# The last stage of a four-layer network: the first weighted addition moved from VectorE to ScalarE and GpSimd

## The reference

```python
xf = layernorm(x).reshape(T, d)                          # T = 4096 tokens, d = 256
shared = silu(xf @ Sg) * (xf @ Su) @ Sd
probs = softmax(xf @ Wr); topk_p, topk_i = top_k(probs, 2)
routed = sum over the two chosen experts e of topk_p * (silu(xf @ Wg[e]) * (xf @ Wu[e]) @ Wd[e])
x = x + routed + shared
```

## Time and profile before

| What | us |
|---|---|
| Median of three executions | 1652.86 (1652.83 to 1653.16) |
| The profiled execution's own time | 1644.97 |
| Its span, from first to last instruction | 1643.2 |
| The last stage in it, from SP's first load to the end | 1587.25 to 1643.2 |
| VectorE busy in the span | 1018.6 |
| ScalarE busy in the span | 736.6 |
| GpSimd busy in the span | 572.3 |

### The profile page before, as it was taken

One profiled execution on the slowest core, in us unless ns is written; L12 is line 12 of the kernel. 1 busy time (PEld: TensorE's weight loads), 2 busy tenths in 40 slices (PEclk: granted clock), 3 DMA queues, 4 the chain that ended last, 5 costly groups with the idle time before them and its releaser, 6 DMA issues. The chain is left out here.

```text
span 1643.2 us, 31228 instructions
## 1 busy us (share of the span) xinstructions
PE 1487.4 (91%) x9905; PEld 1114.3 (68%) x9905; DVE 1018.6 (62%) x3468; ACT 736.6 (45%) x1544; POOL 572.3 (35%) x994
## 2 busy tenths in 40 slices
PE   5999999983999999699799999999999597589987
PEld 3776676772999999565566666666666386468876
DVE  3345555453444444499898888888886286645558
ACT  3444444430222222345177777777777242244420
POOL 4123333344222222245532332322333165635530
PEclk9999999986999999899899999999999798889999
DMA  7001111115777777668857666667761575745556
GB/s 234 1 26 36 49 46 52 39 58 157 212 212 213 212 212 212 211 229 259 203 75 98 98 90 90 92 89 98 98 89 40 143 240 187 171 129 156 161 159 220
DMA packets 150592, 221.74 MB, mean 135 GB/s; under 512 B 23648, under 2 KB 98144, under 8 KB 150304
## 3 DMA queue, kind: packets, MB, share of 16 engines
q1 hardware_dynamic: 127904, 170.58, 45.2%
q0 software_dynamic: 13344, 36.55, 6.4%
q10 hardware_dynamic: 9184, 12.61, 2.5%
HBM read 141.16 MB, written 78.25 MB: 134 GB/s over the span
## 5 line engine op out<-in xcount | busy, mean ns | idle before, releaser
L2095 ACT ACTIVATE t_probs<-t_ps_st 128x512 f32<-128x512 f32 x576 | 313.2, 597 | 124.9 <-PE t_ps_st L2147 122.4
L2073 DVE CUSTOM_DVE_ANT_0 whole_sum<-t_ps_s,t_later 128x512 bf16<-128x512 f32 (+3 forms) x512 | 285.5, 586 | 14.0 <-PE t_ps_s L2133 11.9
L2049 POOL TENSOR_SCALAR_AFFINE_SELECT t_probs<-t_probs 128x128 f32<-128x128 f32 x512 | 137.4, 300 | 330.5 <-ACT t_probs L2095 328.9
L2133 PE MATMUL t_ps_s<-t_ks,t_qs 96*128 96x512 f32 (+3 forms) x768 | 247.8, 362 | 0.5 <-ACT t_neg_max L2085 0.5
L2147 PE MATMUL t_ps_st<-t_qs,t_ks 128*128 128x512 f32 (+3 forms) x768 | 242.7, 365 | 0.8 <-ACT t_probs L2095 0.8
L2147 PEld LDWEIGHTS t_ps_st<-t_qs,t_ks 128*128 128x128 f32 x768 | 136.8, 189 | 73.6 <-ACT t_probs L2095 40.2
L2073 DVE CUSTOM_DVE_ANT_0 whole_sum<-t_ps_s,t_later,t_first_max 128x512 bf16<-128x512 f32 (+3 forms) x256 | 140.5, 549 | 47.8 <-PE t_ps_s L2133 47.8
L2162 PE MATMUL t_ps_o<-t_probs,t_vs 128*17 128x256 f32 (+1 forms) x2560 | 154.9, 361 | 0.5 <-ACT whole_sum L2102 0.5
L2133 PEld LDWEIGHTS t_ps_s<-t_ks,t_qs 96*128 96x128 f32 x768 | 138.7, 190 | 18.0 <-DVE t_first_max L2073 1.6
L1460 POOL DMA_INDIRECT outputs_dram<-m_y,m_place x71 | 68.1, 959 | 208.8 <-DVE m_place L1535 201.1
L1490 PE MATMUL m_ps_h<-m_xt,m_w_t 128*128 128x128 f32 x1136 | 140.7, 278 | 0.0
(11 more groups left out here) (340 smaller groups left out, 2652.1 us busy)
## 6 DMA issues: line engine op xcount, KB each, us to landing
m_w_t<-in_w_dram SPq DMA_DIRECT2D x71, 512.0 KB, 4.4
t_qs<-qkt_dram SPq DMA_DIRECT2D x128, 128.0 KB, 5.6
t_ks<-qkt_dram SPq DMA_DIRECT2D x128, 128.0 KB, 5.7
m_x_t<-gathered_dram SPq DMA_DIRECT2D x79, 128.5 KB, 2.1
m_x_t<-gathered_dram SPq DMA_DIRECT2D x71, 129.0 KB, 2.1
d_ye<-outputs_dram SPq DMA_DIRECT2D x8, 1024.0 KB, 8.2
qkt_dram<-d_hi ACTq DMA_DIRECT2D x32, 256.0 KB, 5.2
qkt_dram<-d_lo SPq DMA_DIRECT2D x32, 256.0 KB, 7.2
```

Source lines behind the costliest of these rows:

```text
L2049: nc.gpsimd.affine_select(out=diag, in_=diag, compare_op=ALU.is_ge, fill=0.0, base=0, pattern=[[1, P]], channel_multiplier=-1).then_inc(ma ...
L2073: nc.vector.tensor_tensor_reduce(out=seen[:, (NP * p + x) % (RS + 1), 0:keys], in0=bank_of(p, x)[:, 0:keys], in1=masks, scale=1.0, scalar= ...
L2095: nc.scalar.activation(probs[:, p % 2, i // NST, base:base + STC], ps_st[(NX * p + i) % RT][:], ACT.Exp, scale=HD ** -0.5).then_inc(exp_re ...
L2133: nc.tensor.matmul(bank_of(p, x)[:, 0:keys], q[0:MAX_ROW, head, qc * P:(qc + 1) * P], k[0:MAX_ROW, head, k0:k0 + keys], start=True, stop=T ...
```

## The change

ScalarE multiplies the first expert's rows of every group by their probability, in place in `ye`, one ACTIVATE (Copy with a scale per partition) per tile: 32 in all. GpSimd, which gets an instruction list in this stage, adds the two tiles' products to `total` in one instruction of 128x512 per group: 16 in all. VectorE has the 32 instructions of L2683 no more; its second additions wait for GpSimd's sum of the same group in the place of the loads and of its own first additions. ScalarE's list is sigmoid k, products of the plain group k, products of the shared group 8 + k - 1.

```diff
--- before.py
+++ after.py
@@ -2648,6 +2648,7 @@
     ps_y = [pb(f"f_ps_y{s}", [P, G, DM]) for s in range(2)]
     g_done, u_done, y_done, sig_ready, gated, h_ready, one_added, two_added, summed = (sem("f_" + n) for n in (
         "g_done", "u_done", "y_done", "sig_ready", "gated", "h_ready", "one_added", "two_added", "summed"))
+    scaled = sem("f_scaled")
     loaded = [sem(f"f_loaded{s}") for s in range(R)]
     stored = [sem(f"f_stored{s}") for s in range(2)]
 
@@ -2677,15 +2678,10 @@
             def add_up(g):
                 q = turn[g]
                 shared = g >= SHARED_BACK
-                dve.wait_ge(loaded[q % R], 32 * (q // R) + 32)
-                for j in range(G):
-                    t = g * G + j
-                    nc.vector.scalar_tensor_tensor(out=total[:, t, :], in0=ye[:, q % R, 0, j, :], scalar=kept["prob"][:, t, 0:1],
-                                                   in1=total[:, t, :], op0=ALU.mult, op1=ALU.add).then_inc(one_added, 1)
+                dve.wait_ge(one_added, q + 1)
                 wait(dve, stored[q % 2], 16 * (q // 2))
                 for j in range(G):
                     t = g * G + j
-                    dve.wait_ge(one_added, G * q + j + 1)
                     nc.vector.scalar_tensor_tensor(out=total[:, t, :] if shared else y[:, q % 2, j, :], in0=ye[:, q % R, 1, j, :],
                                                    scalar=kept["prob"][:, t, 1:2], in1=total[:, t, :], op0=ALU.mult, op1=ALU.add).then_inc(two_added, 1)
                 if shared:
@@ -2702,12 +2698,34 @@
                 if live(k - 1):
                     add_up(SHARED_BACK + k - 1)
 
+        @block.gpsimd
+        def _(pool):
+            for q in range(NG):
+                these = total[:, order[q] * G:(order[q] + 1) * G, :]
+                pool.wait_ge(scaled, G * q + G)
+                nc.gpsimd.tensor_tensor(these, these, ye[:, q % R, 0], ALU.add).then_inc(one_added, 1)
+
         @block.scalar
         def _(act):
-            for k in range(NS):
+            def sigmoid(k):
                 act.wait_ge(g_done, k + 1)
                 wait(act, gated, k - 1)
                 nc.scalar.activation(sig[:, k % 2], ps_g[k % 2][:], ACT.Sigmoid).then_inc(sig_ready, 1)
+
+            def scale_first(g):
+                q = turn[g]
+                act.wait_ge(loaded[q % R], 32 * (q // R) + 32)
+                for j in range(G):
+                    nc.scalar.activation(ye[:, q % R, 0, j, :], ye[:, q % R, 0, j, :], ACT.Copy,
+                                         scale=kept["prob"][:, g * G + j, 0:1]).then_inc(scaled, 1)
+
+            for k in range(NS + 1):
+                if live(k):
+                    sigmoid(k)
+                if k < SHARED_BACK:
+                    scale_first(k)
+                if live(k - 1):
+                    scale_first(SHARED_BACK + k - 1)
 
         @block.sync
         def _(sp):
```

## The result

The changed kernel is slower. Over 18 executions of each kernel in the same sessions the median is 1659.72 us against 1654.96, the ratio 1.003 (1.002 to 1.004): 5.0 us, 3.3 to 6.6. The forecast was 1654.5 with +1.6 for the change, its range ended at 1658.8. Of the 5.2 us between forecast and result 2.1 are the kernel before's own: its median of three executions was 1652.86, that of eighteen is 1654.96. The rest, 3.1, is the change: +4.8 between the medians, where +1.6 was forecast. With the base of the eighteen the same range would have reached 1660.9 and held the result, with two of its terms still off by more than 1 us.

The account below looks back on a forecast made before the run. The prediction took the stores' loop to bound the long rounds and VectorE's work the others. Rounds +2.8 and end -1.2 made +1.6 on 1644.97 us, plus 7.9 carried over: 1654.5 us, range 1648.8 to 1658.8.

Parts of the forecast that it names:

- the bound on the stores' loop: Last stage: a place of `y` turns over in 2.0 us plus the store's way, making three of five rounds long.
- the clash of L2689 with the GpSimd sums: Last stage: a GpSimd sum gets between a pair's two VectorE additions, costing 1.1 us, taken once for each pair.
- ScalarE's part: Last stage: four products per round, 1.9 us beside a 0.60 us sigmoid in at least 5.2, cost nothing in throughput.
- tied to the landings: Last stage: loads and store issued together set off GpSimd's sum and VectorE's pair, so they meet again at every awaited store.
- The end: From the last gate to the end: the last sum begins at 5.7 instead of 6.93 us, -1.2 us.
- The rounds: Rounds 2 to 6 of the last stage: 34.1 us against 31.29, +2.8 us.
- upper edge: Slow side of the forecast's own range, 1652.5 to 1656.8 us: round 2 clashing twice, GpSimd sums of 1.3 us.
- The start to the gate of round 2: Rounds 0 and 1 of the last stage: bound by the gate projections and the first store, change 0.
- the rival of bunched stores: Last stage: clashes, and stores stay bunched; two of four rounds take 7.9 us; +4.4, 1657.3 us; chance 0.21.
- The rival without clashes: Last stage: no clash that counts, stores space out evenly, four rounds at 5.4 us; -4.7, 1648.2 us; chance 0.17.
- the base: Whole kernel before: profiled execution of 1644.97 us, with the runs' median 7.9 above it carried over.

Follow-up runs that it names:

- e4: The kernel before with four places in `y` instead of two; stage 50.8 us, ratio 0.9948 to the kernel before.
- e11: The kernel before with the store put ahead of the loads in SP's queue; stage 50.2 us, ratio 0.9977 to the kernel before.
- e2: The changed kernel without closing GpSimd drain, GpSimd's sums replaced by memsets with the same waits; stage 54.5 us, ratio 0.9981 to the kernel before.
- e6: The kernel before without closing drain, plus 16 GpSimd additions on scratch tiles that nobody waits for; stage 60.2 us, ratio 1.0027 to the kernel before.
- e10: The changed kernel profiled once more, nothing altered; stage 60.8 us, rounds 2 to 6 35.73 us.
- e5: Half the change on the kernel before: ScalarE makes the products, VectorE adds them, GpSimd does nothing; stage 55.6 us, ratio 1.0004.
- e7: The changed kernel without closing GpSimd drain and with four places in `y`; stage 50.0 us, ratio 0.9970 to the kernel before.
- e3: The changed kernel without closing drain, GpSimd's sum of q also waiting for VectorE's pair of q - 2; stage 55.4 us, ratio 0.9987 to the kernel before.
- e9: The kernel before profiled once more, nothing altered; stage 54.8 us, rounds 2 to 6 30.30 us.

## Why the prediction was wrong

The mechanism was right and is shown: the bound on the stores' loop (e4, e11), the clash of L2689 with the GpSimd sums at 1.0 each (e2, e6), its return in the same pairs (e10), ScalarE's part at nothing (e5). That the clash is tied to the landings is shown only in part: five of the nine long pairs had just waited for a store, and in e7 seven pairs are long though none waits for one. There the first pair waits for GpSimd's first sum, and the second sum of the round starts right behind that one. Four of the prediction's sizes were wrong.

The end. The prediction had -1.2 there; measured is -0.2 in the first profile and +0.1 in the mean of two against two. VectorE's part of that term held nearly: the last sum began 5.9 us after the last gate (6.35 in e10), against 5.7 predicted and 6.93 before. The step that failed is an edit that I cost at nothing without naming its cover: GpSimd gets an instruction list in this block. Its closing drain of 7.84 us was in the trace of before, hidden beside the stage from 1587.2 on; with work on GpSimd until 1651.2 it becomes the last to finish, 0.8 to 0.9 us behind the rest.

The rounds. Predicted +2.8, measured +3.7 in the first profile, and +4.6 in the mean of two against two, so this term was mis-sized by more than the end. Half a microsecond of that is the base, whose rounds took 30.30 in its second profile. Round 2 took 8.72 for the 8.1 predicted, because it had no single clash but 2.48 in a pair, both halves blocked by two sums back to back. I had this as an upper edge only. In e10 it took 8.46 with one clash, behind a store's way of 5.41 for 5.13. The start to the gate of round 2, predicted at 0, was 14.6 us for 14.4.

The four rounds 3 to 6 took 26.3 against 26.0, but by two errors that offset each other. I took a clash of 1.1 us for each pair and 3.4 us for each way. Nine pairs of sixteen clashed, but among them all those of the even places in rounds 2 to 6, whose loop bounds these rounds. Three of the four came out at 6.2, with a clash of 1.0 and a way of 3.2 to 3.3, and one at 7.59, behind a way of 4.57. In e10 two of the four were long (7.35 with a way of 4.32, and 7.61 with a way of 5.62 and no clash), together 27.3. That is what the rival of bunched stores said, two long rounds of four, though it had them at 7.9. At +4.4 it also came nearest in size (+3.8 in the first profile, +4.9 in the mean of two). I had given it a chance of 0.21 only.

The rival without clashes, priced at -4.7 us, was too good: e2 has none, and its stage is 0.3 to 1.5 us shorter than the two profiles of before, by its last part. The stores did not space themselves out when VectorE grew lighter; they had to be given places or a better place in the queue.

And the base: three executions within 0.3 us gave a median 2.1 us away from that of eighteen, so that I carried a level over as if it were known to tenths.

What stays open: what makes some of the ways 4.6 to 5.6 us and others 3.2 to 3.4, in e2 as in the kernel before, and why a level of the whole kernel differs by up to 10 us between executions in the stages ahead, which no run here touches.

## What to carry to other kernels

Ask before lightening an engine what it waits for: here its waits for stores took up most of what it gained (e2), while exchanging two lines of SP's loop (e11) or two more places (e4) gave 4 to 6 us of the stage. Work moved to GpSimd that reads SBUF beside VectorE instructions with two SBUF inputs can give much of the time back as waiting inside these, 1.0 us here each time, which a profile counts as busy time; events that both follow made them meet again and again, and one more wait on GpSimd (e3) kept most of them apart; check whether VectorE is on the path there. An engine that gets its first work in a block also moves its closing instructions behind that work.

## What the hardware showed unexpectedly

The closing GpSimd drain of the last block takes 7.84 us in the profiles in which GpSimd has no work there (before, e9, e4, e5, e11), and in the changed kernel it ends 7.86 us after GpSimd's last sum, in both profiles. With the reading DMAs moved behind the storing one on the same queue, a store's way fell by 0.5 us in the median and the longest by 2 (2.9 and 3.8 against 3.4 and 5.8). The DMA engines kept 316 GB/s over a round of 5.2 us in e4 (0.97 busy).
